# Contracting each coordinate broadcast over its own 64 partitions in a deformable gather

## Chip, cores and metric

One core of one Trainium2 chip. The metric is the time of one execution of the whole program on the device, in microseconds (us).

## What is computed

A chain of four layers on x of shape (8, 256, 32, 32) in float32, each added to its input: a selective scan layer, a layer of eight experts, a block of three deformable gathers with convolutions between them, and a wide matrix product. Only the gathers are touched. In the reference each of them is:

```python
py = jnp.clip(yy + off[:, :, 0], 0.0, H - 1)
px = jnp.clip(xx + off[:, :, 1], 0.0, W - 1)
...
v00, v01, v10, v11 = (g(y0, x0), g(y0, x1), g(y1, x0), g(y1, x1))
return v00*(1-wy)*(1-wx) + v01*(1-wy)*wx + v10*wy*(1-wx) + v11*wy*wx
```

So every output pixel of every channel reads its channel's 32x32 image at a fractional place (py, px), with bilinear weights. There are 256 channels in the first gather and 64 in the second and third, each for 8 images.

## The kernel before, in words

`build_gather` (L1286) does the bilinear read as matrix products. The weight of image row r for a pixel is max(0, 1-|py-r|), and likewise for columns. Its work is cut into steps, one for 4 channels and 512 pixels. 32 channels are a block, 4 blocks (UNITS) a set, and 16 blocks a turn of the outer loop (L1298): 4 sets x 2 halves of the pixels x 8 groups of 4 channels x 4 blocks = 256 steps. The first gather has 4 turns, the second and the third 1 each: 6 turns, 1536 steps.

A step has three parts on TensorE and three on other engines:

- `spread_step` (L1374, matmul at L1384): two matmuls, one for each of the two coordinates (y = 0, 1). Each copies the coordinate of 4 channels to 32 partitions each. The operands are `spread` (a matrix of zeros and ones, made in `constants`) and `coord` (the coordinates of one block; partitions 0 to 63 hold the first coordinate, as a high and a low part of 32 partitions each, 64 to 127 the second one). They write two neighbouring banks of PSUM, of 512 values per partition each. For coordinate y the rows of `spread` outside its own 64 partitions are zero.
- ScalarE (L1349) takes |coordinate - index| of both banks at once into `wts`, and VectorE (L1361) takes min(.,1)-1 of it.
- `rows_step` (L1389, matmul at L1397): one float32 product of `img` (4 channels' images on a diagonal) with the row weights; the trace shows it as two matmul records.
- VectorE (L1369) multiplies its result with the column weights into `prod`.
- `fold_steps` (L1400, matmul at L1408), after every fourth step: sums the 32 partitions of each channel for 4 steps; four float32 products with 32 columns each, at four different column positions, shown as 8 records.

TensorE's order is written out by hand: spread of step i+2, rows of step i, and where i % 4 is 1 the fold of the four steps before. `coord`, `spread` are stored as float32r, `img`, `wts`, `prod` and `fold` as float32. A spread waits until ScalarE has read the bank pair two steps back; rows wait for L1361 and for L1369 of two steps back.

The convolutions between the gathers (`build_middle`, L1523) are written in `stacked_conv` (L1440). Its offset products (float32r, 512 pixels, matmul at L1452) have taps that contract 128 partitions, and then taps that contract 64: these alternate between partitions 0 to 63 and 64 to 127 and between two banks.

Of the kernel before, what the change touches and what calls it, by code (L numbers as in the profile page):

```python
# [19 lines left out]
HALF = 512  # L20
# [8 lines left out]
BLK = 32  # L29
# [11 lines left out]
class Stage:  # L41
# [8 lines left out]
    def sem(self, name):  # L50
        if name not in self.sems:
            self.sems[name] = self.ctx.enter_context(self.nc.semaphore(f"{self.tag}_{name}"))
        return self.sems[name]
# [1232 lines left out]
def build_gather(nc, ps, consts, dense, coords, gathered, blocks, tag):  # L1286
# [4 lines left out]
    with ExitStack() as ctx:  # L1291
        st = Stage(nc, ctx, tag)
        sem = st.sem
        spread, fold, index, img = (consts[name] for name in ("spread", "fold", "index", "img"))
        coord = st.sb("coord", [P, SETS, UNITS, N], F32R)
# [7 lines left out]
        with nc.Fori(0, blocks // (SETS * UNITS)) as turn:  # L1303
            n0 = turn * (SETS * UNITS)
            with nc.Block() as block:

                @block.sync
                def _(sp):
                    def load_coord(s, units, halves, signal):
                        px = slice(halves[0] * HALF, (halves[-1] + 1) * HALF)  # L1310
                        sp.dma_start(coord[:, s, units[0]:units[-1] + 1, px].bitcast(F32),
                                     coords[bass.ds(n0 + s * UNITS + units[0], len(units)), :, :, :, px]
                                     .rearrange("a y s p n -> (y s p) a n")).then_inc(sem(signal), 16)

                    for u in range(UNITS):
                        load_coord(0, [u], [0], f"first_coord_loaded{u}")
                    for s in range(SETS):
                        if s:
                            load_coord(s, range(UNITS), range(NH), f"coord_loaded{s}")
                        src = dense[bass.ds((n0 + s * UNITS) * BLK, UNITS * BLK), :]\  # L1320
                            .rearrange("(g c) (i j) -> c i g j", c=4, j=SIDE)
                        for c in range(4):
                            sp.dma_start(img[c * SIDE:(c + 1) * SIDE, s, :, c * SIDE:(c + 1) * SIDE],
                                         src[c]).then_inc(sem(f"img_loaded{s}"), 16)
                        if s == 0:
                            load_coord(0, range(UNITS), [1], "coord_loaded0")
                    for r in range(SETS * NH):
                        s, j = divmod(r, NH)
                        sp.wait_ge(sem("res_ready"), r + 1)
                        sp.dma_start(gathered[bass.ds((n0 + s * UNITS) * BLK, P), j * HALF:(j + 1) * HALF],  # L1330
                                     res[:, r % 2, :]).then_inc(sem(f"stored{r}"), 16)
                    for r in range(SETS * NH):
                        sp.wait_ge(sem(f"stored{r}"), 16)

                @block.scalar
                def _(act):
                    def evacuate(r):
                        act.wait_ge(sem("folded"), NG * (r + 1))
                        if r >= 2:
                            act.wait_ge(sem(f"stored{r - 2}"), 16)  # L1340
                        nc.scalar.activation(res[:, r % 2, :], ps[:, (6 + r % 2) * HALF:(7 + r % 2) * HALF],
                                             ACT.Copy).then_inc(sem("res_ready"), 1)

                    for i in range(n):
                        act.wait_ge(sem("spread_ready"), i + 1)
                        if i >= WB:
                            act.wait_ge(sem("weighted"), i - WB + 1)
                        lo = 2 * (i % 2) * HALF
                        nc.scalar.activation(wts[:, i % WB, :, :].rearrange("p y n -> p (y n)"), ps[:, lo:lo + 2 * HALF],  # L1349
                                             ACT.Abs, bias=index[:, 0:1]).then_inc(sem("distance_ready"), 1)  # L1350
                        if i % per == 8 and i > per:
                            evacuate(i // per - 1)
                    evacuate(SETS * NH - 1)

                @block.vector
                def _(dve):
                    for i in range(n + 1):
                        if i < n:

                            dve.wait_ge(sem("distance_ready"), i + 1)  # L1360
                            nc.vector.tensor_scalar(wts[:, i % WB, :, :], wts[:, i % WB, :, :], 1.0, -1.0, ALU.min,  # L1361
                                                    ALU.add).then_inc(sem("weights_ready"), 1)
                        if i:
                            k = i - 1
                            dve.wait_ge(sem("weights_ready"), i)
                            dve.wait_ge(sem("rows_summed"), k + 1)
                            if k >= PB:
                                dve.wait_ge(sem("folded"), (k - PB) // UNITS + 1)
                            nc.vector.tensor_tensor(prod[:, k % PB, :], ps[:, (4 + k % 2) * HALF:(5 + k % 2) * HALF],  # L1369
                                                    wts[:, k % WB, 1, :], ALU.mult).then_inc(sem("weighted"), 1)  # L1370

                @block.tensor
                def _(pe):
                    def spread_step(i):  # L1374
                        s, j, g, u = steps[i]
                        if i < UNITS:
                            pe.wait_ge(sem(f"first_coord_loaded{u}"), 16)
                        elif i == per or (s and i % (per * NH) == 0):
                            pe.wait_ge(sem(f"coord_loaded{s}"), 16)
                        if i >= 2:  # L1380
                            pe.wait_ge(sem("distance_ready"), i - 1)
                        for y in range(2):
                            lo = (2 * (i % 2) + y) * HALF
                            ins = nc.tensor.matmul(ps[:, lo:lo + HALF], spread[:, y, g, :],  # L1384
                                                   coord[:, s, u, j * HALF:(j + 1) * HALF],
                                                   start=True, stop=True)
                        ins.then_inc(sem("spread_ready"), 1)

                    def rows_step(i):  # L1389
                        s, j, g, u = steps[i]  # L1390
                        if i % (per * NH) == 0:
                            pe.wait_ge(sem(f"img_loaded{s}"), 64)
                        pe.wait_ge(sem("weights_ready"), i + 1)
                        if i >= 2:
                            pe.wait_ge(sem("weighted"), i - 1)
                        lo = (4 + i % 2) * HALF
                        nc.tensor.matmul(ps[:, lo:lo + HALF], img[:, s, u * NG + g, :], wts[:, i % WB, 0, :], start=True,  # L1397
                                         stop=True).then_inc(sem("rows_summed"), 1)

                    def fold_steps(q):  # L1400

                        r, g = divmod(q, NG)
                        pe.wait_ge(sem("weighted"), UNITS * (q + 1))
                        if g == 0 and r >= 2:
                            pe.wait_ge(sem("res_ready"), r - 1)
                        lo = (6 + r % 2) * HALF
                        for u in range(UNITS):
                            ins = nc.tensor.matmul(ps[u * BLK:(u + 1) * BLK, lo:lo + HALF], fold[:, g, :],  # L1408
                                                   prod[:, (UNITS * q + u) % PB, :], start=(g == 0), stop=(g == NG - 1))
                        ins.then_inc(sem("folded"), 1)  # L1410

                    spread_step(0)
                    spread_step(1)
                    for i in range(n):
                        if i + 2 < n:
                            spread_step(i + 2)
                        rows_step(i)
                        if i % UNITS == 1 and i > UNITS:
                            fold_steps(i // UNITS - 1)
                    fold_steps(n // UNITS - 1)  # L1420
# [466 lines left out]
```

## Time and profile before

| | before |
|---|---|
| median of 3 runs | 6671.31 us (6658.63 to 6683.49) |
| profiled execution, first to last instruction | 6663.4 us |
| the six gather turns, warm part of one | about 416 us |
| TensorE matmuls busy, whole program | 5906.7 us (89%) |
| VectorE busy | 4273.1 us (64%) |
| ScalarE busy | 2369.6 us (36%) |
| mean granted TensorE clock, whole program | 0.924 |

The profile is one execution. PE is TensorE's matmuls, PEld its weight loads (LDWEIGHTS), DVE is VectorE, ACT is ScalarE. A matmul's record runs from its issue to the end of its result, so records of neighbouring matmuls overlap. In shapes like `64*128` the first number is the partitions that are contracted, and the second the columns of the stationary operand.

### The profile page before, as it was taken

How to read it: one execution, taken by the hardware profiler on the slowest of the kernel's cores; microseconds unless marked ns; L12 is line 12 of the kernel's file. 1: busy time of each engine (PE TensorE's matmuls, PEld its weight loads, DVE VectorE, ACT ScalarE, POOL GpSimd, SP SyncE). 2: the span in 40 equal slices, each digit the busy share in tenths (PEclk: the TensorE clock that was granted, in tenths of full speed). 3: DMA queues.
4: the chain of work that ended last, by engine and by line, in shares of the span. 5: the costliest groups of instructions: out<-in, count | busy, mean ns of one | idle time of the engine just before them, and what ended most of it. 6: DMA issues, size and time to landing. Idle time of an engine off the chain costs nothing. (4 is left out here: it accounts for less than half of the span.)

```text
span 6663.4 us, 63932 instructions
## 1 busy us (share of the span) xinstructions
PE 5906.7 (89%) x22480; PEld 3405.5 (51%) x22528; DVE 4273.1 (64%) x6238; ACT 2369.6 (36%) x2515; POOL 348.5 (5%) x193
## 2 busy tenths in 40 slices
PE   4877888769998999898997999999999969978997
PEld 2333333247776776676774444444444434434442
DVE  5888888856655665221223777778778747746774
ACT  2222222022221221000001666666666626634651
POOL 0222222300000000000000000000000000000000
PEclk7888888679998999999998999999999989989997
DMA  0000000010000000222124002011020060044012
GB/s 27 19 20 19 20 19 19 13 64 13 13 7 20 13 13 24 88 51 64 45 57 108 5 5 69 5 30 46 5 69 5 5 161 23 5 62 95 6 36 84
DMA packets 237972, 242.27 MB, mean 36 GB/s; under 512 B 176425, under 2 KB 178025, under 8 KB 236745
## 3 DMA queue, kind: packets, MB, share of 16 engines
q1 hardware_dynamic: 237640, 237.98, 13.1%
q8 instruction: 193, 3.16, 0.2%
q14 instruction: 139, 1.13, 0.1%
HBM read 137.28 MB, written 100.66 MB: 36 GB/s over the span
## 5 line engine op out<-in xcount | busy, mean ns | idle before, releaser
L1349 ACT ACTIVATE g_wts<-ps,l_index 128x1024 f32<-128x1024 f32 x1536 | 1712.0, 1115 | 1812.3 <-PE ps L1384 1810.4
L1397 PE MATMUL ps<-g_wts,l_img 128*128 128x512 f32 x3072 | 1577.8, 595 | 19.2 <-DMA l_img<-dense 19.1
L1384 PE MATMUL ps<-g_coord,l_spread 128*128 128x512 f32 x3072 | 1479.9, 563 | 107.6 <-DMA g_coord<-coords 106.3
L1369 DVE TENSOR_TENSOR g_prod<-ps,g_wts 128x512 f32<-128x512 f32 x1536 | 1062.7, 692 | 538.2 <-issue 439.5
L1361 DVE TENSOR_SCALAR g_wts<-g_wts 128x1024 f32<-128x1024 f32 x1536 | 1050.4, 684 | 76.2 <-ACT g_wts L1349 76.2
L1384 PEld LDWEIGHTS ps<-g_coord,l_spread 128*128 128x128 f32 x3072 | 556.9, 191 | 986.0 <-issue 567.6
L1279 PE MATMUL ps<-o_pad,o_ow 128*128 128x512 f32 x3456 | 849.9, 408 | 7.7 <-DVE o_pad L821 7.7
L1092 PE MATMUL ps<-l_pair,l_w 128*128 128x512 f32 x3072 | 782.1, 404 | 0.0
L1279 PEld LDWEIGHTS ps<-o_pad,o_ow 128*128 128x128 f32 x3456 | 657.0, 190 | 195.0 <-DVE o_pad L821 7.9
L1397 PEld LDWEIGHTS ps<-g_wts,l_img 128*128 128x128 f32 x3072 | 577.4, 189 | 170.7 <-DMA l_img<-dense 23.4
L1092 PEld LDWEIGHTS ps<-l_pair,l_w 128*128 128x128 f32 x3072 | 576.6, 191 | 157.0 <-issue 29.4
L751 PE MATMUL ps<-l_rows_p,l_sel 72*128 72x512 bf16 x768 | 293.1, 472 | 211.3 <-DVE l_dbx L608 124.7
L1037 DVE TENSOR_TENSOR l_act<-ps,l_act 128x512 f32<-128x512 f32 x256 | 177.0, 691 | 401.0 <-ACT l_act L965 400.6
L965 ACT ACTIVATE l_act<-ps 128x512 f32<-128x512 f32 x256 | 153.2, 598 | 779.0 <-PE ps L1092 779.0
L1408 PE MATMUL ps<-g_prod,l_fold 128*32 128x512 f32 x3072 | 409.1, 605 | 5.0 <-DVE g_prod L1369 5.0
L1104 PE MATMUL ps<-l_mixed,l_w 128*128 128x512 f32 x1536 | 401.7, 397 | 3.4 <-DVE l_mixed L821 1.9
L1130 DVE SCALAR_TENSOR_TENSOR o_pos<-ps,o_ob,o_grid 128x1024 f32<-128x1024 f32 x32 | 41.1, 1283 | 471.2 <-PE ps L1279 471.2
L1104 PEld LDWEIGHTS ps<-l_mixed,l_w 128*128 128x128 f32 x1536 | 288.2, 188 | 79.2 <-issue 7.3
L427 POOL TENSOR_TENSOR l_acc<-l_acc,l_seen 128x1024 f32<-128x1024 f32 x112 | 283.1, 2528 | 513.6 <-DVE l_seen L618 513.6
L612 DVE TENSOR_TENSOR_SCAN l_states<-ps,l_dbx 128x1024 f32<-128x1024 f32 x128 | 293.2, 2291 | 23.5 <-PE ps L751 19.5
L751 PEld LDWEIGHTS ps<-l_rows_p,l_sel 72*128 72x128 bf16 x768 | 72.9, 109 | 436.3 <-DVE l_dbx L608 167.4
L129 POOL TENSOR_TENSOR l_moments<-l_moments,l_minus_half 128x2 f32<-128x2 f32 x24 | 16.6, 691 | 4302.5 <-DVE l_moments L98 4302.5
(240 smaller groups left out, 4312.7 us busy)
## 6 DMA issues: line engine op xcount, KB each, us to landing
coords<-o_parts SPq DMA_DIRECT2D x192, 256.0 KB, 3.8
g_coord<-coords SPq DMA_DIRECT2D x18, 2048.0 KB, 9.6
l_x<-xcur SPq DMA_DIRECT2D x16, 1024.0 KB, 6.3
l_img<-dense SPq DMA_DIRECT2D x96, 128.0 KB, 6.4
gathered<-g_res SPq DMA_DIRECT2D x48, 256.0 KB, 2.0
l_xn<-in_x SPq DMA_DIRECT2D x8, 1024.0 KB, 4.9
l_acc<-in_x SPq DMA_DIRECT2D x8, 1024.0 KB, 4.9
xcur<-l_acc SPq DMA_DIRECT2D x16, 512.0 KB, 2.8
```

Of the source, the lines that this page charges most:

```text
L427: ins = nc.gpsimd.tensor_tensor(acc[:, h, :], acc[:, h, :], seen[:, i % 2, :], ALU.add)
L612: nc.vector.tensor_tensor_scan(states[:, i % 2, :], ps[:, 0:2 * HALF], dbx[:, i % 2, :], 0.0, ALU.mult, ALU.add).then_inc(sem("da_used"), 1)
L751: ins = nc.tensor.matmul(ps[:, lo:lo + HALF], sel[:, q, :], rows_p[:, mine, h, j * HALF:(j + 1) * HALF], start=True, stop=True)
L1092: ins = nc.tensor.matmul(bank(b_ + i % 2), w[:, a, k, e, f * P:(f + 1) * P], pair[:, m % 2, c, k, j * HALF:(j + 1) * HALF], start=(k == 0 ...
L1104: ins = nc.tensor.matmul(bank(5 + c), w2[:, a, f, e, c * P:(c + 1) * P], mixed2[:, i % 3, d, :], start=(e == 0 and f == 0 and r == 0), sto ...
L1279: ins = nc.tensor.matmul(ps[:, lo:lo + HALF], ow[:, a, kk, tap, y, k * P:(k + 1) * P], padded_rows(pad[:, m, c, kk], j, tap), start=(n == ...
L1349: nc.scalar.activation(wts[:, i % WB, :, :].rearrange("p y n -> p (y n)"), ps[:, lo:lo + 2 * HALF], ACT.Abs, bias=index[:, 0:1]).then_inc( ...
L1361: nc.vector.tensor_scalar(wts[:, i % WB, :, :], wts[:, i % WB, :, :], 1.0, -1.0, ALU.min, ALU.add).then_inc(sem("weights_ready"), 1)
L1369: nc.vector.tensor_tensor(prod[:, k % PB, :], ps[:, (4 + k % 2) * HALF:(5 + k % 2) * HALF], wts[:, k % WB, 1, :], ALU.mult).then_inc(sem(" ...
L1384: ins = nc.tensor.matmul(ps[:, lo:lo + HALF], spread[:, y, g, :], coord[:, s, u, j * HALF:(j + 1) * HALF], start=True, stop=True)
L1397: nc.tensor.matmul(ps[:, lo:lo + HALF], img[:, s, u * NG + g, :], wts[:, i % WB, 0, :], start=True, stop=True).then_inc(sem("rows_summed"), 1)
L1408: ins = nc.tensor.matmul(ps[u * BLK:(u + 1) * BLK, lo:lo + HALF], fold[:, g, :], prod[:, (UNITS * q + u) % PB, :], start=(g == 0), stop=(g ...
```

## The change

Both operands of the spread matmul are cut to the 64 partitions that belong to the coordinate; the rest of that matrix is zero, and the sums are the same. The instructions, their order, their number, their outputs and their semaphores stay as they are.

```diff
                         for y in range(2):
                             lo = (2 * (i % 2) + y) * HALF
-                            ins = nc.tensor.matmul(ps[:, lo:lo + HALF], spread[:, y, g, :],
-                                                   coord[:, s, u, j * HALF:(j + 1) * HALF],
+                            mine = slice(2 * BLK * y, 2 * BLK * (y + 1))
+                            ins = nc.tensor.matmul(ps[:, lo:lo + HALF], spread[mine, y, g, :],
+                                                   coord[mine, s, u, j * HALF:(j + 1) * HALF],
                                                    start=True, stop=True)
                         ins.then_inc(sem("spread_ready"), 1)
```

## Rows read from the trace of the kernel before

**Rows 1.** The page: busy time by engine; the clock granted in 40 slices.

```profile
PE 5906.7 (89%) x22480; PEld 3405.5 (51%) x22528; DVE 4273.1 (64%) x6238; ACT 2369.6 (36%) x2515; POOL 348.5 (5%) x193
PEclk7888888679998999999998999999999989989997
```

**Rows 2.** The page's groups: busy us, mean ns | idle before, releaser.

```profile
L1349 ACT ACTIVATE g_wts<-ps,l_index 128x1024 f32<-128x1024 f32 x1536 | 1712.0, 1115 | 1812.3 <-PE ps L1384 1810.4
L1397 PE MATMUL ps<-g_wts,l_img 128*128 128x512 f32 x3072 | 1577.8, 595 | 19.2 <-DMA l_img<-dense 19.1
L1384 PE MATMUL ps<-g_coord,l_spread 128*128 128x512 f32 x3072 | 1479.9, 563 | 107.6 <-DMA g_coord<-coords 106.3
L1369 DVE TENSOR_TENSOR g_prod<-ps,g_wts 128x512 f32<-128x512 f32 x1536 | 1062.7, 692 | 538.2 <-issue 439.5
L1361 DVE TENSOR_SCALAR g_wts<-g_wts 128x1024 f32<-128x1024 f32 x1536 | 1050.4, 684 | 76.2 <-ACT g_wts L1349 76.2
L1408 PE MATMUL ps<-g_prod,l_fold 128*32 128x512 f32 x3072 | 409.1, 605 | 5.0 <-DVE g_prod L1369 5.0
```

**Rows 3.** Busy us by stretch: PE, PEld, DVE, ACT, POOL; clock, DMA.

```profile
4064.00:4480.00 416.00, 410.91 (x1523) 194.92 (x1521) 327.81 (x508) 284.14 (x260) 0.00 (x0) 1.00 0.09 22
6482.00:6570.00 88.00, 63.08 (x112) 24.91 (x112) 41.18 (x72) 9.63 (x8) 2.76 (x4) 0.71 0.31 106
```

**Rows 4.** Timeline of one period of four steps: start us, duration us, instruction.

```profile
3803.57 1.06 PE L1408 MATMUL ps<-g_prod,l_fold 128*32 128x512 f32 x8
...
3806.46 1.02 PE L1397 MATMUL ps<-g_wts,l_img 128*128 128x512 f32 x2
...
3807.79 1.02 PE L1397 MATMUL ps<-g_wts,l_img 128*128 128x512 f32 x2
3807.99 1.11 ACT L1349 ACTIVATE g_wts<-ps,l_index 128x1024 f32<-128x1024 f32 x1 [0.21 <-PE ps L1384]
3808.19 0.68 DVE L1361 TENSOR_SCALAR g_wts<-g_wts 128x1024 f32<-128x1024 f32 x1
...
3809.11 1.02 PE L1397 MATMUL ps<-g_wts,l_img 128*128 128x512 f32 x2
...
3810.06 1.06 PE L1408 MATMUL ps<-g_prod,l_fold 128*32 128x512 f32 x8
...
3811.06 0.73 PE L1384 MATMUL ps<-g_coord,l_spread 128*128 128x512 f32 x2
...
3811.63 0.59 PE L1397 MATMUL ps<-g_wts,l_img 128*128 128x512 f32 x1
```

**Rows 5.** Timeline in windows narrow enough to show single matmuls of the gather.

```profile
3809.54 0.59 PE L1397 MATMUL ps<-g_wts,l_img 128*128 128x512 f32 x1
...
3811.40 0.39 PE L1384 MATMUL ps<-g_coord,l_spread 128*128 128x512 f32 x1
...
4905.65 0.70 PE L1397 MATMUL ps<-g_wts,l_img 128*128 128x512 f32 x1
```

**Rows 6.** The same in a middle stage: taps of 128, then 64 partitions.

```profile
5377.57 0.41 PE L1452 MATMUL ps<-o_pair,l_ow 128*128 128x512 f32 x1
...
5377.92 0.52 PE L1452 MATMUL ps<-o_pair,l_ow 64*128 64x512 f32 x2
...
5378.27 0.41 PE L1452 MATMUL ps<-o_pair,l_ow 64*128 64x512 f32 x2
...
5379.98 0.41 PE L1452 MATMUL ps<-o_pair,l_ow 64*128 64x512 f32 x2
5380.32 0.65 PE L1625 MATMUL ps<-o_x,l_w 128*64 128x512 f32 x2
```

**Rows 7.** Groups with shapes kept apart, offset products of the middle stages.

```profile
L1452 PE MATMUL ps<-o_pair,l_ow 128*128 128x512 f32 x288 | 78.6, 429 | 7.0 <-DVE o_pair L821 6.9
L1452 PE MATMUL ps<-o_pair,l_ow 64*128 64x512 f32 x288 | 39.5, 415 | 0.0
```

## The prediction

> **What bounds the kernel now.** I read four views, from coarse to fine. The page's chain of waits covers only the last one per cent of the span, in the last stage, so it says nothing of the gathers. The page's busy times [rows 1] put TensorE first with 89% of the span, and its groups [rows 2] say where: the three matmul lines of the gather (1577.8 for the rows, 1479.9 for the spreads, 409.1 for the folds) make up more than half of TensorE's busy time. The reader should look next at what the engines of the gather wait for. ScalarE idles 1810.4 us for the spread matmuls and on nothing else; TensorE's idle time in these three lines is some 130 us over all, nearly all of it for loads at the start of a turn. A stretch of 416 us in the middle of one turn [rows 3] has PE busy 410.91, DVE 327.81 and ACT 284.14 at a granted clock of 1.00 (2.4 GHz). So TensorE is the bound there, and VectorE is next with about four fifths of the stretch.
>
> The timeline [rows 4] shows how TensorE's time is laid out. The pattern repeats every four steps, from fold to fold: 3810.06 - 3803.57 = 6.49 us. Rows of one step start at 3806.46, 3807.79 and 3809.11, that is 1.325 us a step, and the step with a fold in it takes 3811.63 - 3809.11 = 2.52. Together 3 x 1.325 + 2.52 = 6.495, which closes the sum. 384 such periods are 2492 us of the 6663.4 us span. All the rest of the program is untouched.
>
> **How changes of shape show in this trace.** In the plain step nothing is lost between matmuls: the second of two rows matmuls starts 0.43 us after the first (3809.11 to 3809.54, [rows 4, 5]) though each takes 0.59 from issue to result, and a spread matmul takes the array for 0.23 (3811.40 to 3811.63). Where the shape changes from 128x128 to the fold's 128x32, the overlap is gone. The last rows matmul starts at 3809.54 and ends at 3810.13 [rows 5]; the first fold starts at 3810.06 [rows 4], 0.52 after it and not 0.43. This pattern has one answer at every such place: the next shape starts 0.07 us before the last result of the old one. Likewise after the fold: it ends at 3811.12, and the next spread starts at 3811.06. There is a second cost. The first matmul behind a change has its weight load in the open, where other loads run under the matmul ahead: rows directly behind a fold take 0.70 [rows 5], 0.11 more than 0.59. So each change of shape costs 0.09 of emptied array and 0.11 of weight load.
>
> **Do 64 partitions count as a change of shape?** The changed spreads have the shape 64*128. The middle stages have it, in the same float32r, the same 512 columns, alternating halves and two banks [rows 6]. The last 128*128 matmul starts at 5377.57 and ends at 5377.98; the first two 64*128 matmuls start at 5377.92, 0.35 later, where unchanged taps are 0.24 apart (5377.92 is again 0.07 before the end of the old one). The two start together: the row has both within 0.52 us. The next pair starts 0.35 later and takes 0.41, so the first pair took 0.11 for its weight load. The way back is the same: the last pair ends at 5380.39 and the 128*64 shape begins at 5380.32. And the gain of two tiles side by side is there too: 288 matmuls over 128 partitions take 78.6 us and 288 over 64 take 39.5 [rows 7], 0.27 against 0.14 each.
>
> **The change, step by step.** Nothing is removed or moved: the same 3072 spread matmuls and weight loads, the same DMAs and waits. What changes is the time of the pair and what stands at both sides of it. In the plain step there was no change of shape; now there are two, rows to spread and spread to rows.
>
> Plain step after the change, from the first rows matmul of one step to that of the next:
> - the rows' first matmul has its load in the open: +0.11; the second starts 0.43 later; it runs 0.59, and the spreads start 0.07 before its end: 0.11 + 0.43 + 0.59 - 0.07 = 1.06 [rows 4, 5];
> - the pair takes 0.52 as in [rows 6], and the next rows start 0.07 before its end: 0.45.
> Sum 1.51, against 1.325.
>
> Step with a fold: TensorE changes shape there already, into and out of the fold. Now 1.06 to the fold, 1.00 from fold to spread as before (3810.06 to 3811.06, [rows 4]), 0.45 for the pair: 2.51, against 2.52. The one added change is paid by the pair.
>
> Period: 3 x 1.51 + 2.51 = 7.04, against 6.49: +0.55, times 384 is +211 us.
>
> The same in another way, as differences: a plain step gets two changes of 0.09 + 0.11 = 0.20 each and loses one matmul time of 0.23, so 1.325 + 0.40 - 0.23 = 1.495; three of them give +0.51, less 0.01 for the fold step, +0.50 a period and +192 us. Both sums are made of starts printed to 0.01 us; I take the middle, +202 us.
>
> Is anything of this covered? TensorE is the bound, so its added 0.18 a step lies on the path. ScalarE needs 1.11 of a step of 1.5, and VectorE 0.68 + 0.69 = 1.37 [rows 2, 4]; both have room, more than before, and their waits for TensorE grow. No wait is added. A spread starts with its bank pair free: ScalarE reads step i while the spread of i+1 runs and is through some 1.2 us behind the end of spread i, and the spread of i+2 starts 2.5 us behind it. The DMAs at the start of each turn stay as they are, 106.3 us of waits in total [rows 2], and neither gain nor lose.
>
> The sum is made against the profiled execution: 6663.4 + 202 = 6865 for its span; the median of the runs lies 7.9 us above that span, which gives 6873 us.
>
> The Trainium skill speaks on both sides. TensorEngine Tiling (Overview, Theoretical Speedup) gives up to 2x for a contraction of 64 or less; the rows of the middle stages agree for a run of such matmuls, where nothing else stands between them. The same page (Tiling Modes, Key Properties) says that changing the tiling mode drains TensorE. It names no weight load behind the drain, and TensorE: Matmul & The Clock Gate (Part 2, step 1) has loads pulled ahead of matmuls in flight. By the drain alone the time would be that of the first rival; the rows show that the load is not pulled ahead over a change of shape.
>
> **The rivals.**
>
> First, not slower: the weight loads behind a change are hidden here, unlike in the rows. The place is the weight load at both ends of the spread pair. Then rows to spreads is 0.43 + 0.59 - 0.07 = 0.95 and the pair 0.52 - 0.11 - 0.07 = 0.34, the plain step 0.95 + 0.34 = 1.29, the fold step 0.95 + 1.00 + 0.34 = 2.29, and the period 6.16: -0.33 x 384 = -127, 6544 us. If VectorE then holds the plain steps at its 1.37, the period is 3 x 1.37 + 2.29 = 6.40, and the time is 6637. It decides as soon as the two changes of a step cost less than the 0.23 that the pair saves, some 0.11 each. For it: the loads are separate instructions, and no result holds back the one for the rows (VectorE is through at 3808.87, the rows start at 3809.11). Against it: each entry into and exit from a fold in the rows, and the two ends of the 64-partition taps, show the full price.
>
> Second, free changes: two 64-partition matmuls side by side at 0.23 the pair, nothing lost. The plain step would be 1.325 - 0.23 = 1.10 on TensorE, and VectorE would be the bound at up to 1.37: between 1536 x 0.23 = 353 saved, 6318 us, and 3 x 1.37 + 2.29 = 6.40 a period, 6637 us. The rows of the fold speak against it.
>
> Third, the change takes the 64-row shape but the two matmuls do not run side by side (they read one tile each of `coord`, at the same columns): +0.23 a step over the forecast, 353 us, 7226 us. Against it: they write two banks and start together in the middle stage.
>
> Fourth, it does nothing: the array keeps its full shape for the spreads, and the time stays at 6671. Against it: the 64*128 rows.
>
> Fifth, the granted clock falls. The array streams for less of each step: before, 0.43 + 0.43 + 2 x 0.23 = 1.32 of 1.325 us, afterwards 0.43 + 0.43 + 0.23 = 1.09 of 1.51. In the last stage, with PE busy 63.08 of 88 us [rows 3], the mean clock is 0.71. At the lower level (1.2 GHz) a plain step's 1.09 us doubles; if all steps ran so, this would add 1.09 x 1536 = 1674, up to 8547 us. Against it: no wait of TensorE comes in that is longer than a tenth of a microsecond, and the gather ran at 1.00 through its folds.
>
> **How the numbers follow.** Forecast 86%; loads hidden 6%; free changes 1%; not side by side 2%; nothing 2%; clock 3%. The forecast's own range: both sums (192 and 211), 0.02 us of reading error in a plain step (1152 of them, 23 us), and 12 us of spread of the runs before, add up to 6863 - 35 and 6882 + 35; cut where both errors would have to fall together, that is 6835 to 6915. It holds nearly all of the 86%. I give 6835 to 6925, ten more above, for single stretches at the lower clock. What a measurement of this kernel can tell from no change is about 0.5%, 33 us. Faster by more: 7%; within: 2%; slower: 91%.
>
> **What would show it.** Right: in the plain step rows start 1.5 us apart; two spread matmuls start within 0.02 us of each other, 0.52 behind the second rows matmul, and take 0.51 each; the first rows matmul of every step takes 0.70 instead of 0.59; period 7.0 us; ScalarE's wait for L1384 grows by some 200 us (1152 x 0.18); clock 1.00 in the middle of a turn. Wrong: rows of 0.59 behind a spread (loads hidden), starts of the pair 0.2 apart (not side by side), a period of 6.49 with full shapes, or a clock under 1.00 in the middle of a turn.

## The result, and the profile after

The changed kernel takes 6840.68 us (median of 4 runs, 6834.65 to 6848.54), the kernel before 6669.64 beside it (4 runs). The ratio is 1.0256, 95% interval 1.0241 to 1.027: slower by 171 us, where 202 were forecast. It lies inside the forecast range of 6835 to 6925, 6 us above its lower end. The profiled execution spans 6838.4 us.

These are the page's rows of the kernel after that answer to [rows 1, 2]. The change adds a line, so rows are now L1398, spreads L1385 and folds L1409:

```profile
PE 6075.6 (89%) x22528; PEld 3020.1 (44%) x22528; DVE 4272.7 (62%) x6238; ACT 2369.6 (35%) x2515; POOL 348.6 (5%) x193
L1349 ACT ACTIVATE g_wts<-ps,l_index 128x1024 f32<-128x1024 f32 x1536 | 1711.6, 1115 | 1985.2 <-PE ps L1385 1985.1
L1398 PE MATMUL ps<-g_wts,l_img 128*128 128x512 f32 x3072 | 1739.4, 649 | 23.6 <-DMA l_img<-dense 23.6
L1385 PE MATMUL ps<-g_coord,l_spread 64*128 64x512 f32 x3072 | 773.4, 500 | 110.8 <-DMA g_coord<-coords 109.1
L1409 PE MATMUL ps<-g_prod,l_fold 128*32 128x512 f32 x3072 | 409.1, 605 | 5.0 <-DVE g_prod L1369 5.0
```

Taken alone, the spread's row reads like a success: 773.4 us busy in place of 1479.9. The rows' line has grown from 1577.8 to 1739.4 (649 instead of 595 ns for one), and ScalarE's wait for the spreads from 1810.4 to 1985.1, by 174.7: that is the loss, seen from the engine that waits. Busy times of overlapping matmuls don't add up to the time that an engine needs. The distance between starts does, and it stands in the timeline of TensorE (start us, duration us), which answers to [rows 4]:

```profile
4198.06 0.50 PE L1385 MATMUL ps<-g_coord,l_spread 64*128 64x512 f32 x2
4198.49 1.13 PE L1398 MATMUL ps<-g_wts,l_img 128*128 128x512 f32 x2
4199.55 0.50 PE L1385 MATMUL ps<-g_coord,l_spread 64*128 64x512 f32 x2
4199.97 1.12 PE L1398 MATMUL ps<-g_wts,l_img 128*128 128x512 f32 x2
4201.03 0.50 PE L1385 MATMUL ps<-g_coord,l_spread 64*128 64x512 f32 x2
4201.46 1.13 PE L1398 MATMUL ps<-g_wts,l_img 128*128 128x512 f32 x2
4202.52 0.49 PE L1385 MATMUL ps<-g_coord,l_spread 64*128 64x512 f32 x2
4202.94 1.13 PE L1398 MATMUL ps<-g_wts,l_img 128*128 128x512 f32 x2
4204.00 1.06 PE L1409 MATMUL ps<-g_prod,l_fold 128*32 128x512 f32 x8
4204.99 0.50 PE L1385 MATMUL ps<-g_coord,l_spread 64*128 64x512 f32 x2
4205.42 0.70 PE L1398 MATMUL ps<-g_wts,l_img 128*128 128x512 f32 x1
```

Rows start at 4198.49, 4199.97, 4201.46 and 4202.94: a plain step takes 1.483 us, and the one with the fold 4205.42 - 4202.94 = 2.48. A period is 3 x 1.483 + 2.48 = 6.93 against 6.49 [rows 4]; 0.44 x 384 = 169 of the 171 us. (The profile models the ends of matmuls; this sum uses starts alone.) The reader should see three things. A spread pair starts 0.07 us before the two rows end (4198.49 + 1.13 = 4199.62, next 4199.55), and the rows 0.07 before the pair ends, as at every change of shape in the rows of before: the overlap with the matmul ahead is gone. The first rows matmul takes 0.70 (last line) where it took 0.59: its weight load is in the open. And the pair takes 0.50 in all: it does run side by side.

### The profile page after: what moved, and what is told of

It is laid out like the page before. It is cut to its first block and busy times, and to the rows that moved or that the text cites. A ratio compares the mean times of both kernels' runs of the same rounds, so it can differ in the third digit from the quotient of the medians.

```text
span 6838.4 us, 63980 instructions
## 1 busy us (share of the span) xinstructions
PE 6075.6 (89%) x22528; PEld 3020.1 (44%) x22528; DVE 4272.7 (62%) x6238; ACT 2369.6 (35%) x2515; POOL 348.6 (5%) x193
## 3 DMA queue, kind: packets, MB, share of 16 engines
q14 instruction: 138, 1.13, 0.1%
## 5 line engine op out<-in xcount | busy, mean ns | idle before, releaser
L1349 ACT ACTIVATE g_wts<-ps,l_index 128x1024 f32<-128x1024 f32 x1536 | 1711.6, 1115 | 1985.2 <-PE ps L1385 1985.1
L1398 PE MATMUL ps<-g_wts,l_img 128*128 128x512 f32 x3072 | 1739.4, 649 | 23.6 <-DMA l_img<-dense 23.6
L1361 DVE TENSOR_SCALAR g_wts<-g_wts 128x1024 f32<-128x1024 f32 x1536 | 1049.6, 683 | 74.7 <-ACT g_wts L1349 74.7
L1385 PE MATMUL ps<-g_coord,l_spread 64*128 64x512 f32 x3072 | 773.4, 500 | 110.8 <-DMA g_coord<-coords 109.1
L1385 PEld LDWEIGHTS ps<-g_coord,l_spread 64*128 64x128 f32 x3072 | 288.6, 185 | 1311.0 <-issue 887.0
L1398 PEld LDWEIGHTS ps<-g_wts,l_img 128*128 128x128 f32 x3072 | 460.2, 189 | 404.5 <-issue 375.5
L1409 PE MATMUL ps<-g_prod,l_fold 128*32 128x512 f32 x3072 | 409.1, 605 | 5.0 <-DVE g_prod L1369 5.0
```

What stands on the lines that cost most here:

```text
L1385: ins = nc.tensor.matmul(ps[:, lo:lo + HALF], spread[mine, y, g, :], coord[mine, s, u, j * HALF:(j + 1) * HALF], start=True, stop=True)
```

## The experiments

All are edits of the kernel before or after. `same_tile` alone leaves part of the computation out. Times of before are those measured beside each group of runs: 6664.0 for the first four, 6666.3 for the next four, 6663.1 and 6666.2 for the last two groups.

### Is it the change of shape, and are the two tiles the gain?

**One coordinate only** (`one_coord`):

```diff
-                            ins = nc.tensor.matmul(ps[:, lo:lo + HALF], spread[:, y, g, :],
-                                                   coord[:, s, u, j * HALF:(j + 1) * HALF],
+                            mine = slice(0, 2 * BLK) if y == 0 else slice(0, P)
+                            ins = nc.tensor.matmul(ps[:, lo:lo + HALF], spread[mine, y, g, :],
+                                                   coord[mine, s, u, j * HALF:(j + 1) * HALF],
```

> Only the first coordinate's matmul is cut to its 64 partitions, the second keeps 128. Theory (a change of shape costs 0.20 us, and the gain needs two tiles side by side): a plain step has two changes and no gain, 0.43 + 0.52 + 0.42 + 0.34 = 1.71 us, the fold step 2.71, the period of four steps 7.84 against 6.49, so 6670 + 384 x 1.35 = 7188 us. Rival (the loss goes with the number of 64-partition matmuls): half of them, half of the loss, about 6755 us.

Measured: 7204 us (ratio 1.081, 1.0788 to 1.0831). Half as many 64-partition matmuls cost three times as much. TensorE's timeline:

```profile
4200.27 1.02 PE L1398 MATMUL ps<-g_wts,l_img 128*128 128x512 f32 x2
4201.22 0.92 PE L1385 MATMUL ps<-g_coord,l_spread 64*128 64x512 f32 x2
4201.98 1.02 PE L1398 MATMUL ps<-g_wts,l_img 128*128 128x512 f32 x2
4202.93 0.93 PE L1385 MATMUL ps<-g_coord,l_spread 64*128 64x512 f32 x2
```

A plain step is 4201.98 - 4200.27 = 1.71, as the theory said to the hundredth. The pair, one matmul of each shape, takes 0.92, because a change lies between its halves; the rows take 1.02 again, since they follow a matmul of their own shape. The rival that counts narrow matmuls falls. The time is 16 us above the expected 7188; the clock at the starts of the turns is a little lower than in the changed kernel (last section), which is worth about that by an estimate there.

**Both in one tile** (`same_tile`), `mine = slice(0, 2 * BLK)` for both:

> Both matmuls of a pair are cut to partitions 0 to 63; this leaves out the second coordinate (its weights there are zero), the work has the same size. Theory: the two can't run side by side in one tile, so the second starts 0.34 us behind the first, a plain step takes 1.48 + 0.23 = 1.71, and the time is 6841 + 353 = 7194 us. Rival (the pair's gain comes from the shorter contraction, wherever it lies): as after the change, 6841 us.

Measured: 7245 us (1.0871, 1.0849 to 1.0893). The pair is no longer side by side:

```profile
4200.45 0.73 PE L1385 MATMUL ps<-g_coord,l_spread 64*128 64x512 f32 x2
4201.12 1.12 PE L1398 MATMUL ps<-g_wts,l_img 128*128 128x512 f32 x2
4202.17 0.73 PE L1385 MATMUL ps<-g_coord,l_spread 64*128 64x512 f32 x2
4202.84 1.13 PE L1398 MATMUL ps<-g_wts,l_img 128*128 128x512 f32 x2
```

It takes 0.73 instead of 0.50, and a plain step 4202.84 - 4201.12 = 1.72. So a shorter contraction by itself gives nothing; the 0.23 come from two tiles. The run is 51 us above the expectation. Its period is 4199.45 - 4191.58 = 7.87 us from fold to fold, 0.94 more than the changed kernel's 6.93, and 0.94 x 384 = 361. The other some 40 us lie at the starts of the turns, where the clock stays low for longer (last section).

**96 partitions** (`rows96`), `slice(0, 3 * BLK) if y == 0 else slice(0, P)`:

> The first coordinate's matmul is cut to 96 partitions, the second keeps 128. Theory (96 partitions still use the full array's shape): nothing changes, 6670 us, plain step 1.325 us. Rival (any contraction below 128 is a change of shape): 7190 us as with one coordinate in 64.

Measured: 6666.08 us, ratio 1.0005 (0.9995 to 1.0015): the same. TensorE's timeline has the spacing of before (4203.51 to 4204.84 is 1.33), though the matmul is of another size by name:

```profile
4203.51 1.02 PE L1398 MATMUL ps<-g_wts,l_img 128*128 128x512 f32 x2
4203.97 1.03 PE L1385 MATMUL ps<-g_coord,l_spread 96*128 96x512 f32 x2
4204.84 0.59 PE L1398 MATMUL ps<-g_wts,l_img 128*128 128x512 f32 x1
```

So what costs is the tile of 64 partitions between full shapes, and not a contraction of less than 128 as such: 96 partitions cost nothing.

### Where does it pay?

**Only behind a fold** (`behind_fold`), where the shape changes anyway: `mine` is the coordinate's own 64 partitions `if i >= 8 and i % UNITS == 0`, else all. (It is 372 pairs, three fewer than the expectation says.)

> Only the spread pair that stands right behind a fold is cut to 64 partitions (375 of 1536 pairs, those where the shape changes anyway); all others keep 128. Theory: one change added for each, at 0.20, and 0.23 saved: the period goes from 6.49 to 6.46, about -12 us, 6658 us, the same within what a measurement tells. Rival (the price lies in the 64-partition pair, not in added changes): a quarter of the loss, +43 us, 6713 us.

Measured: 6649.47 us over 10 runs against 6664.02, ratio 0.9981 (0.9971 to 0.999): -14.6 us, -12 expected. The profile shows one side of it:

```profile
4202.30 1.02 PE L1398 MATMUL ps<-g_wts,l_img 128*128 128x512 f32 x2
4203.25 1.07 PE L1409 MATMUL ps<-g_prod,l_fold 128*32 128x512 f32 x8
4204.24 0.50 PE L1385 MATMUL ps<-g_coord,l_spread 64*128 64x512 f32 x2
4204.68 1.13 PE L1398 MATMUL ps<-g_wts,l_img 128*128 128x512 f32 x2
...
4206.10 1.02 PE L1398 MATMUL ps<-g_wts,l_img 128*128 128x512 f32 x2
```

From 4202.30 to 4206.10 are 3.80 us, where before it is 2.52 + 1.325 = 3.845 [rows 4]: one pair for 0.50 and one load in the open. The sign of the same edit turns with its place.

**Twice the spreads** (`double_full`, `double_64`): `for y in (0, 1, 0, 1)` in the kernel before and in the one after.

> Every spread pair is issued twice, with 128 partitions as before the change (the second time over the first one's result). Theory: two more matmuls of 0.23 us a step, 6670 + 1536 x 0.46 = 7377 us. It is the other side of the next run.

> Every spread pair is issued twice, with 64 partitions each. Theory (the price is paid once for a run of 64-partition matmuls, and the pairs behind the first cost 0.23): 6841 + 1536 x 0.23 = 7194 us, 180 less than with 128 partitions, where the single pair was 171 slower. Rival (each 64-partition matmul has its weight load in the open): 0.34 a pair, 6841 + 522 = 7363 us.

Measured: 7370.74 us with 128 partitions and 7192.30 with 64. Here the tiles win by 178 us, where the single pair loses 171. In the second kernel

```profile
4202.76 1.13 PE L1398 MATMUL ps<-g_wts,l_img 128*128 128x512 f32 x2
4203.82 0.74 PE L1385 MATMUL ps<-g_coord,l_spread 64*128 64x512 f32 x4
4204.48 1.12 PE L1398 MATMUL ps<-g_wts,l_img 128*128 128x512 f32 x2
```

four matmuls take 0.74, against 0.50 for two: the second pair costs 0.24, and a plain step is 1.72 for work that takes 1.325 + 0.46 = 1.785 with full shapes (1.78 in the timeline of `double_full`). The price is paid once for a run of two pairs; longer runs were not tried in the gather.

### Runs of real work: a kernel that uses the tiles

The doubled work is of no use, but two steps' spreads can stand together. `batch_full` and `batch_64` change the order by hand in TensorE's program, with 128 and 64 partitions:

```diff
-                    for i in range(n):
+                    for i in range(0, n, 2):
                         if i + 2 < n:
                             spread_step(i + 2)
+                            spread_step(i + 3)
                         rows_step(i)
-                        if i % UNITS == 1 and i > UNITS:
+                        rows_step(i + 1)
+                        if i % UNITS == 0 and i > UNITS - 1:
                             fold_steps(i // UNITS - 1)
```

> 128 partitions as before, but TensorE's order is spread, spread, rows, rows for two steps at a time. Theory: TensorE's own work is the same, 6.49 us a period; with two spreads in a row the second may wait for ScalarE's read of its bank pair, so 6670 to 6750 us.

> The same order in twos, with 64 partitions. Theory (price by change of shape): a batch of two steps pays the two changes once: 0.52 + 0.34 + 0.32 + 0.54 + 0.43 + 0.43 = 2.58 us, with a fold 3.58, the period 6.16 against 6.49: 6543 us if nothing else waits, 6605 if VectorE's 1.37 a step holds the plain batch at 2.74. Rival (the order in twos makes the waits, see the run with 128 partitions): not under 6670 us.

Measured: 6769.97 us (1.0151, 1.0134 to 1.0168), above the expected span, and 6664.83 us (0.9999, 0.999 to 1.0009). The tiles bring 105 us from one to the other, but `batch_64` reaches neither 6543 nor 6605. Its timeline shows where it waits:

```profile
4202.24 0.69 DVE L1369 TENSOR_TENSOR g_prod<-ps,g_wts 128x512 f32<-128x512 f32 x1 [1.42 <-issue]
4202.85 0.69 DVE L1361 TENSOR_SCALAR g_wts<-g_wts 128x1024 f32<-128x1024 f32 x1
...
4203.45 0.68 DVE L1369 TENSOR_TENSOR g_prod<-ps,g_wts 128x512 f32<-128x512 f32 x1
4203.60 2.31 PE L1398 MATMUL ps<-g_wts,l_img 128*128 128x512 f32 x4
4204.05 0.68 DVE L1361 TENSOR_SCALAR g_wts<-g_wts 128x1024 f32<-128x1024 f32 x1
4204.79 0.30 PEld L1398 LDWEIGHTS ps<-g_wts,l_img 128*128 128x128 f32 x2 [0.89 <-DVE g_wts L1361]
```

The weights of this batch's second rows are loaded at 4204.79, behind VectorE's min (L1361) that ends at 4204.73. That min is the last of four VectorE instructions back to back, and VectorE idled 1.42 us ahead of the first, the product at 4202.24: in its program order each product stands before the next step's min, and the product's rows come late when TensorE does two steps at a time.

So in the next runs VectorE does the product of step i-2 behind the min of step i (`batch_64_skew`, `batch_full_skew`, with `WB` 6; `batch_64_skew4` with `WB` 4):

```diff
-                    for i in range(n + 1):
+                    for i in range(n + 2):
...
-                        if i:
-                            k = i - 1
-                            dve.wait_ge(sem("weights_ready"), i)
+                        if i > 1:
+                            k = i - 2
+                            dve.wait_ge(sem("weights_ready"), k + 1)
```

> The order in twos with 64 partitions, and VectorE takes its product one step later (min of step i, then the product of step i-2, not i-1), with six instead of four weight buffers. Theory: in the order in twos the rows waited for weights because VectorE stood at a product whose rows were late; with that gone, TensorE's own 6.16 us a period is left: 6670 - 384 x 0.33 = 6543 us. Rival (VectorE has no time for it, or ScalarE's read of the bank pair is what is late): stays near 6665 us.

> The same, with 128 partitions. Theory: TensorE's own work is 6.49 us a period, 6670 us, 100 less than in twos without the later product; the 127 us to the run with 64 partitions are the gain of the tiles alone. Rival (the order in twos costs something by itself): 6700 us and more.

> As the first of this call, with the four weight buffers of before. Theory (the later product is what matters, the buffers are not): within 20 us of it. Rival (ScalarE waits for buffers): 6600 us and more.

Measured: 6623.05 us (0.9939, 0.9922 to 0.9956), 6711.74 (1.0071, 1.0054 to 1.0088) and 6628.35 (0.9946, 0.9926 to 0.9966). VectorE's order brings 42 us with 64 partitions and 58 with 128, where the theory gave 122 and 100. The buffers don't matter. The difference between the two, the gain of the tiles alone in this order, is 89 us and not the expected 127. So both are short of the theory (6543 and 6670), and the full shape in twos stays slower than before: the order in twos does cost something by itself. What is left in `batch_64_skew`:

```profile
4202.78 2.18 PE L1398 MATMUL ps<-g_wts,l_img 128*128 128x512 f32 x4
4204.88 1.07 PE L1409 MATMUL ps<-g_prod,l_fold 128*32 128x512 f32 x8
4205.88 0.73 PE L1385 MATMUL ps<-g_coord,l_spread 64*128 64x512 f32 x4
4206.54 1.99 PE L1398 MATMUL ps<-g_wts,l_img 128*128 128x512 f32 x4
4208.46 0.73 PE L1385 MATMUL ps<-g_coord,l_spread 64*128 64x512 f32 x4
```

The plain batch (4205.88 to 4208.46) takes 2.58 us, its own sum; the rows ahead of the fold take 2.18 instead of 1.99. They follow a plain batch of 2.58 us, in which VectorE works at 1.20 us a step (4202.85 to 4204.05 above, from min to min) and has little slack, while it gets 1 us more where a fold lies in the batch. That reading is tested next. The other engines' lines say what those rows wait for:

```profile
4201.22 0.69 DVE L1361 TENSOR_SCALAR g_wts<-g_wts 128x1024 f32<-128x1024 f32 x1 [1.28 <-ACT g_wts L1349]
...
4203.03 0.68 DVE L1369 TENSOR_TENSOR g_prod<-ps,g_wts 128x512 f32<-128x512 f32 x1
...
4203.83 0.30 PEld L1398 LDWEIGHTS ps<-g_wts,l_img 128*128 128x128 f32 x2 [0.76 <-DVE g_wts L1361]
```

The load at 4203.83 is put down to a min, but its own min had ended at 4203.11. What ends just before it, at 4203.71, is the product at 4203.03. It is that of two steps back, which every rows step waits for as well (see the kernel), and with the later product this wait, no longer the one for the min, comes last. The product is the fourth VectorE instruction back to back, and the first, the min at 4201.22, had waited for ScalarE's first distance of the batch.

**The fold between** (`fold_between`): the fold moves from behind the rows to between the spreads and the rows of every second batch.

```diff
                             spread_step(i + 3)
+                        if i % UNITS == 2 and i > UNITS:
+                            fold_steps(i // UNITS - 1)
                         rows_step(i)
                         rows_step(i + 1)
-                        if i % UNITS == 0 and i > UNITS - 1:
-                            fold_steps(i // UNITS - 1)
```

> As batch_64_skew, and the fold stands between two pairs of spreads and two pairs of rows of every second batch, not behind the rows; its four steps are older by then. The number of changes of shape is the same, five a period. Theory (what is left of the waits is the second rows of a fold batch, 0.12 us late for VectorE): ScalarE and VectorE work on the new steps under the fold, the waits go, and the period falls from 6.35 to 6.16: some 73 us less, about 6550 us. Rival (VectorE's order of min and product holds the chain wherever the fold stands): no change from 6623 us.

Measured: 6546.82 us (0.9819, 0.9803 to 0.9836), 119 us faster than before, 294 faster than the change that it contains; about 6550 were expected. One period:

```profile
4202.03 1.06 PE L1409 MATMUL ps<-g_prod,l_fold 128*32 128x512 f32 x8
4203.02 1.98 PE L1398 MATMUL ps<-g_wts,l_img 128*128 128x512 f32 x4
4204.94 0.73 PE L1385 MATMUL ps<-g_coord,l_spread 64*128 64x512 f32 x4
4205.60 1.98 PE L1398 MATMUL ps<-g_wts,l_img 128*128 128x512 f32 x4
4207.52 0.74 PE L1385 MATMUL ps<-g_coord,l_spread 64*128 64x512 f32 x4
4208.18 1.07 PE L1409 MATMUL ps<-g_prod,l_fold 128*32 128x512 f32 x8
```

It takes 4208.18 - 4202.03 = 6.15 us, the 6.16 that the prices of the prediction give, and both sets of rows take 1.98. So moving the fold takes away the late rows. That the chain through VectorE made them late is read from the trace above and agrees with this run; ScalarE's distance stands at the start of that chain, and its share was not separated. This last order was not run with 128 partitions. Since the work of TensorE alone is 6.49 us a period there, in whatever order, and the kernel before already runs at that, no gain is to be expected from the order without the tiles; but that is argued, not measured.

## Why the prediction was right, point by point

- **The bound.** TensorE in the gather: right. ScalarE's wait rose by 174.7 us with the time.
- **64 partitions are a change of shape.** Right; `one_coord` shows the price without the gain, `rows96` that the tile counts.
- **0.09 for the emptied array and 0.11 for the load, at both ends.** Right. The next shape starts 0.07 us before the last result, the first rows matmul takes 0.70.
- **The pair.** The term that was mis-sized. It was set at 0.52 from the middle stage [rows 6] and measured 0.50 and 0.49. A tap of the middle stage takes 0.41 from issue to result, a spread of the gather 0.39 [rows 5, 6]; with 0.11 for the load that is 0.52 there and 0.50 here. The forecast had both numbers and took the first. The second sum, made with the spread's 0.23, came nearer, and the forecast took the middle of both.
- **Plain step 1.51 or 1.495, measured 1.483; fold step 2.51, measured 2.48.** From rows to spreads it is 1.06 as forecast; from spreads to rows 0.42 to 0.43 instead of 0.45, and from fold to spread 0.99 instead of 1.00. Each step is 0.01 to 0.03 too long. Over 384 periods the first sum is 42 us too long and the second 23, which is the distance between 202 and 171.
- **VectorE's 1.37 a step.** A wrong reading that the forecast did not hang on. It adds up two busy times, but neighbouring instructions of VectorE overlap as TensorE's do. In the kernel before a product and the min behind it start 0.61 apart:

```profile
3810.23 0.69 DVE L1369 TENSOR_TENSOR g_prod<-ps,g_wts 128x512 f32<-128x512 f32 x1
3810.84 0.69 DVE L1361 TENSOR_SCALAR g_wts<-g_wts 128x1024 f32<-128x1024 f32 x1
```

So VectorE needs about 1.2 us a step (1.20 in `batch_64`). The bounds of 6637 us in the first two rivals and of 6605 in the expectation of `batch_64` rest on 1.37 and are too high: `batch_64_skew` runs plain batches of 2.58 us, under twice 1.37.
- **The rivals.** Loads hidden and free changes fall with the 0.70 of the first rows matmul and with the starts 0.07 before the old result; not side by side falls with the pair's 0.50 (0.73 in `same_tile`), no effect with the time itself. The clock was 1.00 in the middle of the turns, 0.925 over the program against 0.924.

The Trainium skill's page TensorEngine Tiling (Array Packing), section Tiling Modes, Key Properties, says that a change of tiling mode drains TensorE. The runs agree, with starts 0.52 us apart instead of 0.43 where the shape changes, and add what a change costs here: with the load in the open 0.20 us, of which the drain is less than half.

## What to carry to other kernels

Before narrowing a contraction to run tiles side by side, count the changes of shape: one costs 0.20 us here (512 columns, full clock), a pair of tiles saves 0.23. A lone pair between full matmuls pays two changes for one saving and loses; a run of two pairs pays them for two and wins. Read the price off neighbouring places of the trace where the shape changes already. Then put narrow matmuls together, next to other changes, and see that the engines fed by them keep up with the new rhythm. Read what an engine needs for a step from start to start where it works back to back, not from the sum of its busy times.

## What was not expected of the hardware

With both narrow matmuls in one tile the clock took longer to rise after the wait for loads at the start of a turn. These are stretches at the same turn of `same_tile` and of the changed kernel (busy us of PE, PEld, DVE, ACT, POOL; granted clock; DMA):

```profile
5208.00:5269.00 61.00, 51.99 (x85) 15.84 (x85) 19.46 (x30) 17.72 (x16) 0.00 (x0) 0.50 0.69 173
```

```profile
4999.00:5061.00 62.00, 50.01 (x158) 15.21 (x158) 34.91 (x54) 31.11 (x28) 0.00 (x0) 0.83 0.71 172
```

TensorE shows some 50 us of busy time in both, yet the clock is at 0.50 (1.2 GHz) throughout the first and 0.83 on average in the second, where it rose after about a third. This turn is the extreme one. Over the first 60 us of each of the six turns the mean granted clock is 0.88 to 0.94 before, 0.87 to 0.90 in the changed kernel, 0.80 to 0.89 in `one_coord` and 0.53 to 0.78 in `same_tile`. Averaged over the turns that is 0.18 less in `same_tile` than in the changed kernel, and 0.18 x 60 x 6 = 65 us of full clock; for `one_coord` it is 0.04, or 14 us. These are estimates; the two profiled runs took some 52 and 12 us beyond what their periods give, which is of that size. Why the clock differs is open: `same_tile` leaves the second half of the array's rows without spread work, but `one_coord` uses them and is lower too, and no run separates the reasons.
